# A list of its own, and operands of their own, for the last batch at the end of an attention and FFN kernel

## The reference, cut to what matters

```python
x = layernorm(x + attention(x, Wqkv, bqkv, Wout, bout))
h = silu(tlin(x, w1_w, w1_s)) * tlin(x, w2_w, w2_s)
h = gelu(tlin(h, h1_w, h1_s))          # 1024 x 1024
h = gelu(tlin(h, h2_w, h2_s))          # 1024 x 1024
x = layernorm(x + tlin(h, w3_w, w3_s))
```

## Time and profile before

| | us |
|---|---|
| median of 3 runs | 2323.64 |
| lowest, highest | 2322.57, 2328.25 |
| the profiled execution, its own time | 2323.13 |
| its span from first to last instruction | 2321.4 |
| PE busy | 2208.8 (95%) |
| ACT busy | 1293.6 (56%) |
| DVE busy | 1278.9 (55%) |

### The profile page before, as it was taken

How to read it: one execution, slowest core, us unless ns; L and a number is a source line. 1 busy time by engine, 2 the same in 40 slices (tenths; PEclk the granted TensorE clock), 3 DMA queues, 4 the chain that set the end, 5 groups by cost and what they waited for, 6 DMA issues and landing times.

```text
span 2321.4 us, 52007 instructions
## 1 busy us (share of the span) xinstructions
PE 2208.8 (95%) x16294; PEld 1871.2 (81%) x16294; DVE 1278.9 (55%) x3961; ACT 1293.6 (56%) x2769; POOL 488.1 (21%) x896
## 2 busy tenths in 40 slices
PE   4758999999999999999999999999999999999998
PEld 2336888888888888888888888888888888888898
DVE  4564565555556556555655556565555656555433
ACT  1334566565656656565665656656565565656543
POOL 1121222122222212212221222212122221222211
PEclk7779999999999999999999999999999999999999
DMA  8642223232232323223232232323223232312000
GB/s 288 209 142 63 66 59 74 55 76 60 63 71 59 75 55 71 65 61 71 61 75 55 67 69 61 70 61 75 55 61 75 59 69 64 75 42 50 23 6 10
DMA packets 96838, 166.18 MB, mean 72 GB/s; under 512 B 21568, under 2 KB 40768, under 8 KB 96576
## 3 DMA queue, kind: packets, MB, share of 16 engines
q1 hardware_dynamic: 88736, 139.02, 25.9%
q10 hardware_dynamic: 7840, 23.86, 3.0%
HBM read 93.08 MB, written 71.83 MB: 71 GB/s over the span
## 4 chain that ended last, share of the span: by engine, by line
PE 77%; DMA 4%; issue 3%; SPq 3%; ACT 2%; DVE 2%; POOL 0%; ACTq 0%; DVEq 0%; POOLq 0%
PE ring L1055 38%; PE ring L1041 8%; PE pM L951 6%; PE pO L973 6%; PE pS L939 6%; PE ring L1068 5%; PE ring L985 4%; PE ring L1021 2%; DMA dn<-den_d 2%; DMA qk_d<-c 2%; PE ring L1005 1%; SPq L504 1%; DVE full_g L805 1%; PE ring L959 1%; ACT L698 1%
## 5 line engine op out<-in xcount | busy, mean ns | idle before, releaser
L766 DVE CUSTOM_DVE_ANT_0 pM<-pM,mask 128x512 f32<-128x512 f32 (+3 forms) x1024 | 493.4, 507 | 318.7 <-PE pM L951 262.5
L1055 PE MATMUL ring<-Xhi,H 128*128 128x256 f32 x2048 | 515.4, 291 | 6.6 <-ACT full_h L711 5.0
L1055 PE MATMUL ring<-Yhi,H 128*128 128x256 f32 x2048 | 507.4, 285 | 0.0
L1055 PE MATMUL ring<-Ylo,H 128*128 128x256 f32 x2048 | 502.8, 283 | 0.0
L1055 PE MATMUL ring<-Xlo,H 128*128 128x256 f32 x2048 | 499.3, 282 | 0.0
L1055 PEld LDWEIGHTS ring<-Xhi,H 128*128 128x128 f32 x2048 | 391.1, 191 | 18.7 <-ACT full_h L711 11.7
L1055 PEld LDWEIGHTS ring<-Ylo,H 128*128 128x128 f32 x2048 | 390.9, 191 | 3.2
L1055 PEld LDWEIGHTS ring<-Xlo,H 128*128 128x128 f32 x2048 | 392.1, 191 | 1.1
L1055 PEld LDWEIGHTS ring<-Yhi,H 128*128 128x128 f32 x2048 | 390.2, 191 | 2.6
L951 PE MATMUL pM<-Ks,Qs 128*128 128x512 f32 x992 | 297.4, 358 | 48.4 <-DMA Ks<-qk_d 31.4
L710 ACT ACTIVATE Yhi<-ring,cols 128x256 fp32r<-128x256 f32 x256 | 120.8, 472 | 285.8 <-PE ring L1055 251.2
(11 more groups left out here) (102 smaller groups left out, 3336.8 us busy)
## 6 DMA issues: line engine op xcount, KB each, us to landing
qk_d<-c SPq DMA_DIRECT2D x124, 256.0 KB, 3.4
Qs<-qk_d SPq DMA_DIRECT2D x124, 192.0 KB, 4.4
Ks<-qk_d SPq DMA_DIRECT2D x124, 192.0 KB, 4.9
qk_d<-c SPq DMA_DIRECT2D x124, 128.0 KB, 3.1
xTs<-in_xT SPq DMA_DIRECT2D x16, 512.0 KB, 4.4
raw<-in_h ACTq DMA_DIRECT2D x8, 1024.0 KB, 24.5
xz<-in_x SPq DMA_DIRECT2D x16, 512.0 KB, 6.5
Oc<-Osb SPq DMA_DIRECT2D x256, 32.0 KB
```

Source lines behind the costliest of these rows:

```text
L766: nc.vector.tensor_tensor_reduce(pM[:, h % 2, 0:n], pM[:, h % 2, 0:n], mask[:, T - n:T], 1.0, NEG, ALU.add, ALU.max, mx[:, t, h:h + 1]).th ...
L1055: mm = nc.tensor.matmul(to, w, x_part, start=(k == 0 and m == 0), stop=(k == KB - 1 and m == 1))
```

## The change

The change concerns iterations 16 and 17 alone.

1. A table `TAIL_ORDER` takes the place of what was left of `ORDER` in iteration 16, and iteration 17 has no step left. It has banks of its own, numbered in turn over the steps that are really there. Nothing is added or dropped: it is the same work in another order. In it `ln1` and the two `x1_turn` steps stand among the `h2` blocks of batch 14, `gu` of half 0 and of half 1 follow one another (with batch 14's `ffn_out` after the second block), then come h1 of half 0, h1 of half 1, h2 of half 0, h2 of half 1, and the two `ffn_out`. The last block of `h2` of half 1 stands after the first part of half 0's `ffn_out`.
2. Half 0 of batch 15 gets tiles of its own, `Xhi_t`, `Xlo_t`, `Yhi_t`, `Ylo_t`, laid over `Qs`, `Ks` and `probs_a`, whose last reader is the attention of batch 15. `operands` chooses.
3. `u_of` numbers batch 15 layer by layer, and the waits on `h_lo` and `h_full` follow it. `ffn_hi` of batch 15's half 0 no longer waits for `f_ready`.

```diff
+TAIL_ORDER = """
+y:-1:0:0 y:-1:0:1 y:-1:1:0 y:-1:1:1 h2:-2:1:0:0 h2:-2:1:0:1 h_act:-2:h2:1:0 h_rest:-2:h2:1:0 ln1_stats:-1
...
+h_rest:-2:h2:1:7 gu:-1:0:0 gu:-1:0:1 ffn_out:-2:1:0 ffn_hi:-1:0:0 ffn_out:-2:1:1 gu:-1:0:2 ffn_hi:-1:0:1
+gu:-1:0:3 ffn_hi:-1:0:2 gu:-1:0:4 ffn_hi:-1:0:3 ln2_stats:-2:1 gu:-1:0:5 ffn_hi:-1:0:4 ln2:-2:1 gu:-1:0:6
...
+TAIL = plan(TAIL_ORDER)
+TAIL_BANKS = ring_banks(TAIL)
...
+    if i is not None and i >= B:
+        return TAIL if i == B else []
...
-    return HEAD_BANKS if steps is HEAD else BANKS
+    return HEAD_BANKS if steps is HEAD else TAIL_BANKS if steps is TAIL else BANKS
...
+        Xhi_t, Xlo_t = (over(nc, q_at + n * KB * HALF * 4, name, [P, KB, HALF], F32R) for n, name in enumerate(("Xhi_t", "Xlo_t")))
+        Yhi_t = over(nc, k_at, "Yhi_t", [P, KB, HALF], F32R)
...
+        Ylo_t = over(nc, p_at, "Ylo_t", [P, KB, HALF], F32R)
...
-        def u_of(kind, half, j):
-            return (2 * half + (kind == "h2")) * KB + j
+        def is_last(b):
+            return isinstance(b, int) and b == B - 1
+
+        def u_of(b, kind, half, j):
+
+            second = kind == "h2"
+            return ((half + 2 * second) if is_last(b) else (2 * half + second)) * KB + j
+
+        def operands(b, half):
+
+            return (Xhi_t, Xlo_t, Yhi_t, Ylo_t) if is_last(b) and half == 0 else (Xhi, Xlo, Yhi, Ylo)
...
-                        need(act, f_ready, b * 2 + half)
-                        nc.scalar.activation(Xhi[:, j], full_g[:, j % 2], ACT.Copy).then_inc(x_hi, 1)
+                        if not is_last(b):
+                            need(act, f_ready, b * 2 + half)
+                        elif half:
+                            act.wait_ge(f_ready, b * 2)
+                        nc.scalar.activation(operands(b, half)[0][:, j], full_g[:, j % 2], ACT.Copy).then_inc(x_hi, 1)
...
-                        s, n = (x_lo, b * (2 * KB) + (half + 1) * KB) if kind == "h1" else (h_lo, b * 32 + half * 16 + KB)
+                        s, n = ((x_lo, b * (2 * KB) + (half + 1) * KB) if kind == "h1" else
+                                (h_lo, b * 32 + u_of(b, "h1", half, KB - 1) + 1))
```

More of the change, by code:

```diff
@@ L146 @@
 """
+TAIL_ORDER = """
+y:-1:0:0 y:-1:0:1 y:-1:1:0 y:-1:1:1 h2:-2:1:0:0 h2:-2:1:0:1 h_act:-2:h2:1:0 h_rest:-2:h2:1:0 ln1_stats:-1
+h2:-2:1:1:0 h2:-2:1:1:1 h_act:-2:h2:1:1 h_rest:-2:h2:1:1 h2:-2:1:2:0 h2:-2:1:2:1 h_act:-2:h2:1:2
+h_rest:-2:h2:1:2 ln1:-1 h2:-2:1:3:0 h2:-2:1:3:1 h_act:-2:h2:1:3 h_rest:-2:h2:1:3 h2:-2:1:4:0 h2:-2:1:4:1
+h_act:-2:h2:1:4 h_rest:-2:h2:1:4 x1_turn:-1:0 h2:-2:1:5:0 h2:-2:1:5:1 h_act:-2:h2:1:5 h_rest:-2:h2:1:5
+x1_turn:-1:1 h2:-2:1:6:0 h2:-2:1:6:1 h_act:-2:h2:1:6 h_rest:-2:h2:1:6 h2:-2:1:7:0 h2:-2:1:7:1 h_act:-2:h2:1:7
@@ new lines @@
+h_act:-1:h1:0:1 h_rest:-1:h1:0:1 h1:-1:0:2:0 h1:-1:0:2:1 h_act:-1:h1:0:2 h_rest:-1:h1:0:2 h1:-1:0:3:0
+h1:-1:0:3:1 h_act:-1:h1:0:3 h_rest:-1:h1:0:3 h1:-1:0:4:0 h1:-1:0:4:1 h_act:-1:h1:0:4 h_rest:-1:h1:0:4
+h1:-1:0:5:0 h1:-1:0:5:1 h_act:-1:h1:0:5 h_rest:-1:h1:0:5 h1:-1:0:6:0 h1:-1:0:6:1 h_act:-1:h1:0:6
+h_rest:-1:h1:0:6 h1:-1:0:7:0 h1:-1:0:7:1 h_act:-1:h1:0:7 h_rest:-1:h1:0:7 h1:-1:1:0:0 h1:-1:1:0:1
+h_act:-1:h1:1:0 h_rest:-1:h1:1:0 h1:-1:1:1:0 h1:-1:1:1:1 h_act:-1:h1:1:1 h_rest:-1:h1:1:1 h1:-1:1:2:0
@@ new lines @@
+h2:-1:0:3:0 h2:-1:0:3:1 h_act:-1:h2:0:3 h_rest:-1:h2:0:3 h2:-1:0:4:0 h2:-1:0:4:1 h_act:-1:h2:0:4
+h_rest:-1:h2:0:4 h2:-1:0:5:0 h2:-1:0:5:1 h_act:-1:h2:0:5 h_rest:-1:h2:0:5 h2:-1:0:6:0 h2:-1:0:6:1
+h_act:-1:h2:0:6 h_rest:-1:h2:0:6 h2:-1:0:7:0 h2:-1:0:7:1 h_act:-1:h2:0:7 h_rest:-1:h2:0:7 h2:-1:1:0:0
+h2:-1:1:0:1 h_act:-1:h2:1:0 h_rest:-1:h2:1:0 h2:-1:1:1:0 h2:-1:1:1:1 h_act:-1:h2:1:1 h_rest:-1:h2:1:1
+h2:-1:1:2:0 h2:-1:1:2:1 h_act:-1:h2:1:2 h_rest:-1:h2:1:2 h2:-1:1:3:0 h2:-1:1:3:1 h_act:-1:h2:1:3
@@ L149, in plan @@
+h_rest:-1:h2:1:3 h2:-1:1:4:0 h2:-1:1:4:1 h_act:-1:h2:1:4 h_rest:-1:h2:1:4 h2:-1:1:5:0 h2:-1:1:5:1
+h_act:-1:h2:1:5 h_rest:-1:h2:1:5 h2:-1:1:6:0 h2:-1:1:6:1 h_act:-1:h2:1:6 h_rest:-1:h2:1:6 ffn_out:-1:0:0
+h2:-1:1:7:0 h2:-1:1:7:1 h_act:-1:h2:1:7 h_rest:-1:h2:1:7 ffn_out:-1:0:1 ln2_stats:-1:0 ln2:-1:0 ffn_out:-1:1:0
+ffn_out:-1:1:1 ln2_stats:-1:1 ln2:-1:1
+"""
 def plan(order):
@@ L275, in build @@
         xz = sb("xz", [P, 2, TB, C])
+        p_at = nc.sbuf_base
         probs_a = sb("probs_a", [P, PAIRS, 2, T])
+        Ylo_t = over(nc, p_at, "Ylo_t", [P, KB, HALF], F32R)
         probs_b = sb("probs_b", [P, PAIRS, 2, T - P])
@@ L574, in work @@
                         pool.wait_ge(x_hi, b * (2 * KB) + half * KB + j + 1)
-                        nc.gpsimd.tensor_tensor(Xlo[:, j], full_g[:, j % 2], Xhi[:, j].bitcast(F32),
+                        hi, lo, _, _ = operands(b, half)
+                        nc.gpsimd.tensor_tensor(lo[:, j], full_g[:, j % 2], hi[:, j].bitcast(F32),
                                                 ALU.subtract).then_inc(x_lo, 1)
@@ L701, in work @@
                         kind, half, j = a
-                        u = u_of(kind, half, j)
+                        u = u_of(b, kind, half, j)
                         act.wait_ge(h_ready, b * 32 + u + 1)
@@ L706, in work @@
                         if kind == "h1":
-                            hi, sc = Yhi[:, j], sh1_c[:, j:j + 1]
+                            hi, sc = operands(b, half)[2][:, j], sh1_c[:, j:j + 1]
                         else:
-                            hi, sc = Xhi[:, j], sh2_c[:, j:j + 1]
+                            hi, sc = operands(b, half)[0][:, j], sh2_c[:, j:j + 1]
                         nc.scalar.activation(hi, src, ACT.Gelu, scale=sc)
@@ L809, in work @@
                         layer, half, j = a
-                        u = u_of(layer, half, j)
+                        u = u_of(b, layer, half, j)
                         dve.wait_ge(h_full, b * 32 + u + 1)
-                        hi, lo = (Yhi[:, j], Ylo[:, j]) if layer == "h1" else (Xhi[:, j], Xlo[:, j])
-                        nc.vector.tensor_tensor(lo, full_h[:], hi.bitcast(F32), ALU.subtract).then_inc(h_lo, 1)
+                        hi, lo = operands(b, half)[2:] if layer == "h1" else operands(b, half)[:2]
+                        nc.vector.tensor_tensor(lo[:, j], full_h[:], hi[:, j].bitcast(F32), ALU.subtract).then_inc(h_lo, 1)
                     elif kind == "rec_save":
@@ L916, in bank @@
                         last, last_off, last_a = taken[n]
-                        s, per, nth = RELEASE[last](*last_a)
-                        pe.wait_ge(s, (i + last_off) * per + nth)
+                        if last in ("h1", "h2"):
+                            pe.wait_ge(h_full, (i + last_off) * 32 + u_of(i + last_off, last, *last_a) + 1)
+                        else:
+                            s, per, nth = RELEASE[last](*last_a)
+                            pe.wait_ge(s, (i + last_off) * per + nth)
                     taken[n] = (kind, off, a)
@@ L1046, in iteration @@
                         half, j, part = a
-                        W, src = (H1, (Xhi, Xlo)) if kind == "h1" else (H2, (Yhi, Ylo))
-                        s, n = (x_lo, b * (2 * KB) + (half + 1) * KB) if kind == "h1" else (h_lo, b * 32 + half * 16 + KB)
+                        W, src = (H1, operands(b, half)[:2]) if kind == "h1" else (H2, operands(b, half)[2:])
+                        s, n = ((x_lo, b * (2 * KB) + (half + 1) * KB) if kind == "h1" else
+                                (h_lo, b * 32 + u_of(b, "h1", half, KB - 1) + 1))
                         to = bank(kind, off, (half, j), part == 0)[:, 0:HALF]
@@ L1064, in iteration @@
                             if t == 0 and k in (0, KB // 2, KB - 1):
-                                pe.wait_ge(h_lo, b * 32 + half * 16 + 2 * KB - {0: 4, 4: 1, 7: 0}[k])
-                            for m, X in enumerate((Xhi, Xlo)):
+                                pe.wait_ge(h_lo, b * 32 + u_of(b, "h2", half, KB - 1) + 1 - {0: 4, 4: 1, 7: 0}[k])
+                            for m, X in enumerate(operands(b, half)[:2]):
                                 w, x_part = parts(W3[:, k], X[:, k, tok])
```

12 lines of the change are left out of this document (10 added, 2 removed).

## The result

The changed kernel took 2316.94 us (median of 8 runs, 2313.47 to 2319.8), the kernel before 2325.15 us in its 8 runs (2322.57 to 2328.25). The ratio is 0.997, with a 95% interval of 0.9961 to 0.9978: 0.30% faster, or 7.0 us, where 8.5 us had been forecast. The interval runs from 5.1 to 9.1 us, and the two medians lie 8.2 us apart, so the times alone show a gain but can't tell 7.0 from 8.5. What was right and wrong in the forecast has to be read from the profiles.

What follows compares the result with a forecast made beforehand. PE was taken as the bound. Losses of 2.75 + 4.93 + 2.14 + 1.19 = 11.0 us, less 2.0 and 0.6 of new cost, plus 0.1, gave 8.5 us: 2323.13 - 8.5 = 2314.6 us, range 2312.0 to 2318.0.

Steps and rivals of the forecast that it cites:

- Step 2: `gu` and first `h1` block of half 0: 4.93 us lost, 2.8 of it to the slow clock, all to be regained.
- The transposes: Between batch 14's `ffn_out` and `gu`: two PE waits lose 2.75 us, all regained by placing the transposes among `h2`.
- The joints of gate and up with `h1`: From `gu` to the first `h1` block: 4.93 us lost at half 0, 2.14 at half 1; waits for `Xlo` go.
- the bank of the last `h1` block: Half 1's `h1` blocks 6 and 7 share a bank: 1.19 us lost, regained by numbering in turn.
- DVE's new wait: Sixteen `gu` blocks in a row: PE waits 2.0 us for DVE, about 1.2 and 0.8, at half 1's first two blocks.
- The late scale of half 1: At the very end: half 1's scale queues behind DVE's work for half 0 and begins 0.6 us later.
- The first rival: The clock falls in PE's new wait for PSUM banks among `gu`; at most 2.8 us, time 2317.4 us; chance 0.12.
- Everything ahead of 2194.81 stays: Before PE's first `y` matmul of iteration 16: nothing changes, leaving some 126 us in play.
- a change of that stretch as a sign of being wrong: The stretch up to `y` at 2194.81 us: if it changed, the prediction would be wrong.
- The joints between halves: `h1` to `h1` and `h1` to `h2` of two halves: no loss there before, so nothing to win.

Runs made afterwards that it cites:

- `ln2_late`: Changed kernel with batch 14's second layer norm moved from the gate and up blocks to among half 0's `h1` blocks; ratio 0.9964, end 115.9 us.
- `turn_back`: Changed kernel with `ln1`, both `x1_turn` and batch 14's `ffn_out` back ahead of `gu`; ratio 0.998, ends 121.2, 119.7 and 119.8 us.
- `halves_in_turn`: Changed kernel with half 0's FFN wholly ahead of half 1's, and batch 14's `ln2` among the `h1` blocks; ratio 0.997, end 118.1 us.
- `banks_only`: Kernel before with only the banks of its last two iterations numbered in turn over the steps left; ratio 0.9987, end 121.8 us.

## Why the prediction was right and wrong

**Where it failed: the clock, as a term of the sum.** Step 2 charged 2.8 us for the slow matmuls between `gu` and `h1` to the time of before, as if each execution paid them, and the forecast gave all of it back as gain. The row was right for its execution, and the size for one full fall too (126.6 - 123.9 = 2.7). But the fall comes in three of eight profiles, and twice only half as long. On average it costs 0.7 us. With 0.7 in place of 2.8 the forecast's own sum is 6.4 us; the profiles give 124.6 - 117.6 = 7.0, and so does the ratio. All the other terms were of the right size or a little too cautious. The clock did stay up in the changed kernel, as forecast; what failed is the price put on its fall before. Why it falls in some executions only isn't known.

**The transposes** (2.75 us): right. Before, 3.85 us lay between `ffn_out` and `gu`; now the blocks of `h2` on either side of a transpose are 2214.72 - 2212.36 = 2.36 us apart instead of 1.92, as ACT's gelus after them show, so two cost 0.9. The gain is 3.0. The 0.9 is what the forecast had put at 1.1, the transposes' own time; its caution about tenths lost between kinds of matmul wasn't needed.

```profile
2212.36 0.47 ACT L766 ACTIVATE Xhi<-ring,cols 128x256 fp32r<-128x256 f32 x1 [1.08 <-PE ring L1113]
...
2214.72 0.47 ACT L766 ACTIVATE Xhi<-ring,cols 128x256 fp32r<-128x256 f32 x1 [1.03 <-PE ring L1113]
```

**The joints of gate and up with `h1`, and the bank of the last `h1` block** (4.93 - 2.8 = 2.1, 2.14, and 1.19): right in sum. At full clock 3.0 + 2.1 + 2.1 + 1.2 = 8.4 stand against 2.2 us of new cost, which leaves 6.2, and 6.3 are measured (123.9 - 117.6). The two joints were not measured one by one.

**DVE's new wait** (2.0 us, in two pieces of 1.2 and 0.8 at blocks 0 and 1 of half 1): right in place, number and cause, a little too long. By starts they are 2231.34 - 2230.17 - 0.12 = 1.05 and 0.53, in sum 1.6 us. `ln2_late` showed the cause.

**The late scale of half 1** (0.6 us): right. The last matmul starts at 2308.69, so without the queue the scale would start 0.16 after its slot, at 2308.97; it starts at 2309.53, 0.56 later.

**The first rival**, that the clock falls in DVE's new wait: no. The stretches around it have 1.00 in both profiles of the changed kernel; the three of `turn_back` have the same two waits, and no fall there either. The Trainium skill, "TensorE: Matmul & The Clock Gate", section "A second HAM failure mode: psum-queue depth-cycling", describes the clock going to and fro with short idle times between groups of matmuls. In this kernel the clock fell once and came back at the transposes of before, in some executions, and not at the new wait for banks, where PE was busy for 2.73 of 4.00 us. The forecast weighed this for the new wait and never for the old one, which was the one that mattered.

**The level of the time.** The forecast of 2314.6 us is `y` at 2194.81, an end of 126.6 - 8.5 = 118.1, and the 1.7 us beyond the span. The end came out at 117.6, so this part was right to 0.5 us. The median was 2316.94, 2.3 above the forecast, because 2194.81 was the earliest `y` of eight, where the average is 2198.3. The forecast made no correction for the profiled execution, which turned out to be 2.0 us below the median of the eight runs (2325.15). Two things in it were not typical, and hid each other in part: an early `y` (3.5 us) and a full fall of the clock (2.0 us above the average). "Everything ahead of 2194.81 stays" is true of the work and not of the time. The prediction named a change of that stretch as a sign of being wrong; it did move, by scatter. The range gave such scatter no room of its own.

**The alternation.** The forecast held the joints between halves for hidden already, and said that there was nothing to win at `h1` to `h2`; no wait of PE stands there in the kernel before. What the alternation saves are the two joints from gate and up to `h1`, where `halves_in_turn` has 1.4 us of waits for `Xlo`. The change gives most of that back by DVE's new wait (1.6 us) and the late scale (0.56), and is 0.5 us ahead in all.

## What to carry to other kernels

A loss to the clock that one profile shows may be a draw and not a constant, as it was here. Before it is put into a forecast as gain, take a second profile of the kernel before; if it can't be had, forecast with and without it. When a hand-written order is cut at the end of a pipeline, number its buffers anew over the steps that are left: here that gave a third of the gain at full clock for a few lines. And whoever closes up one engine's work should look for small jobs of another that had lived in the gaps: 2.1 us of layer norm among gate and up cost 1.7 us of PE, and nothing among the `h1` blocks behind it.

## What the runs showed of the hardware that was not expected

- The same waits of PE, 1.24 and 1.41 us around four transposes, were followed by a granted clock of half for 28 matmuls, for about 15, or not at all (one, two and five of eight profiles). One wait of 1.9 us behind eight transposes was so in one of four profiles (`turn_back` three times, `banks_only` once).
- The stretch from the first to the last reading of the softmax sums took 2041.4 to 2051.1 us in eight profiles of the same kernel, a scatter larger than the effect under study.
